# Filter spectra in memory as slot pairs instead of channel chunks, in a two-layer graph kernel on one core

## The reference

```python
# layer 0
norm  = (sum(adj, -1) + 1e-6) ** -0.5
f_hom = (adj @ ((x @ theta) * norm)) * norm
gate  = sigmoid(x @ W_t + b_t)
x     = layernorm(x + elu(gate * f_hom + (1 - gate) * (x @ W_h)))
# layer 1, xc = x with nodes last
h      = relu(bn1(conv1d(xc, conv1_w, 0)))
h      = bn2(conv1d(h, conv2_w, 8))          # 256 -> 256 channels, 17 taps
x_conv = relu(h + xc)
...                                          # A = exp(-dist), x_nmp = A @ relu(x @ w_msg.T + b_msg)
x      = layernorm(x + gru(concat(x_conv, x_nmp), x))
```

## Time and profile before

| | |
|---|---|
| median of 3 runs | 2163.93 us (2160.73 to 2166.66) |
| the profiled execution | 2163.51 us, span 2161.7 us |
| phase_a | from 0 to about 545 us |
| phase_spectrum | about 545 to 767 us |
| phase_product | about 767 to 985 us |
| phase_c | about 985 us to the end |

### The profile page before, as it was taken

One profiled execution on the slowest core, in us unless ns is written; L12 is line 12 of the kernel. 1 busy time (PEld: TensorE's weight loads), 2 busy tenths in 40 slices (PEclk: granted clock), 3 DMA queues, 4 the chain that ended last, 5 costly groups with the idle time before them and its releaser, 6 DMA issues.

```text
span 2161.7 us, 36678 instructions
## 1 busy us (share of the span) xinstructions
PE 1971.6 (91%) x11270; PEld 1695.5 (78%) x11270; DVE 1583.6 (73%) x2837; ACT 1245.1 (58%) x2303; POOL 425.1 (20%) x370
## 2 busy tenths in 40 slices
PE   6888888887788879994999999999999999999997
PEld 5887777776688868883888888888888888888886
DVE  5999798798577766774777677777777777777674
ACT  6887687786455566663445454545454545545452
POOL 5887687685000000000000000000000000000000
PEclk9999999998899989996999999999999999999999
DMA  4556566555322268884212121212122121212110
GB/s 145 204 200 209 192 225 218 198 207 218 91 82 79 72 207 263 255 265 152 76 52 92 46 91 45 91 46 90 60 77 77 59 81 55 88 49 91 62 40 20
DMA packets 174943, 263.25 MB, mean 122 GB/s; under 512 B 13250, under 2 KB 125608, under 8 KB 170632
## 3 DMA queue, kind: packets, MB, share of 16 engines
q1 hardware_dynamic: 174856, 262.29, 35.9%
HBM read 174.16 MB, written 88.08 MB: 121 GB/s over the span
## 4 chain that ended last, share of the span: by engine, by line
PE 51%; issue 1%; DVE 1%; DMA 1%; ACT 1%; SPq 0%; POOLq 0%; POOL 0%; ACTq 0%; DVEq 0%
PE c_ps_g L1431 37%; PE c_ps_m L1412 4%; PE c_ps_s L1412 2%; PE c_ps_m L1440 2%; PE c_ps_y L1466 1%; PE c_ps_m L1442 1%; PE c_ps_y L1510 1%; PE c_ps_m L1510 1%; PE c_ps_s L1494 1%; PE c_ps_m L1441 1%; DMA c_yf<-y_spec 1%; PE c_ps_m L1511 0%; PE c_ps_y L1511 0%; DVE c_wi_l L1377 0%; ACT c_yo L1143 0%
## 5 line engine op out<-in xcount | busy, mean ns | idle before, releaser
L1215 POOL TENSOR_TENSOR c_rstd<-c_var_eps,c_neg_half 128x4 f32<-128x4 f32 x32 | 32.2, 1008 | 1131.7 <-DVE c_var_eps L1331 1131.7
L1431 PE MATMUL c_ps_g<-c_xh,c_wh_l 128*128 128x512 f32 x384 | 155.3, 405 | 0.0
L1431 PE MATMUL c_ps_g<-c_nh,c_wi_l 128*128 128x512 f32 x384 | 153.3, 399 | 0.0
L1431 PE MATMUL c_ps_g<-c_xl,c_wh_h 128*128 128x512 f32 x384 | 151.8, 395 | 0.0
L1431 PE MATMUL c_ps_g<-c_xh,c_wh_h 128*128 128x512 f32 x384 | 151.7, 395 | 0.0
L1431 PE MATMUL c_ps_g<-c_ch,c_wi_l 128*128 128x512 f32 x384 | 151.6, 395 | 0.0
L1431 PE MATMUL c_ps_g<-c_ch,c_wi_h 128*128 128x512 f32 x384 | 151.6, 395 | 0.0
L1431 PE MATMUL c_ps_g<-c_nh,c_wi_h 128*128 128x512 f32 x384 | 151.5, 395 | 0.0
L1431 PE MATMUL c_ps_g<-c_cl,c_wi_h 128*128 128x512 f32 x384 | 151.5, 395 | 0.0
L1431 PE MATMUL c_ps_g<-c_nl,c_wi_h 128*128 128x512 f32 x384 | 151.5, 395 | 0.0
L837 PE MATMUL m_ps<-m_wh,m_xl 128*128 128x256 f32 (+1 forms) x406 | 131.8, 325 | 20.7 <-DVE m_wl L817 20.6
(11 more groups left out here) (228 smaller groups left out, 6658.9 us busy)
## 6 DMA issues: line engine op xcount, KB each, us to landing
w_spec<-a_spec SPq DMA_DIRECT2D x32, 1088.0 KB, 11.0
m_w<-w_spec SPq DMA_DIRECT2D x34, 1024.0 KB, 7.5
a_xt<-in_x_t SPq DMA_DIRECT2D x64, 256.0 KB
a_xn<-in_x_n SPq DMA_DIRECT2D x64, 256.0 KB, 9.4
x_t<-a_x1t SPq DMA_DIRECT2D x64, 256.0 KB, 9.5
s_x<-x_t SPq DMA_DIRECT2D x64, 256.0 KB, 3.0
y_spec<-m_y SPq DMA_DIRECT2D x64, 256.0 KB, 5.6
c_x<-x_t SPq DMA_DIRECT2D x32, 512.0 KB, 4.1
```

Of the source, the lines that this page charges most:

```text
L1431: last = nc.tensor.matmul(out, stationary, moving, start=(count == 0), stop=(count == total - 1))
```

## The change

The scratch tensor becomes (34 pairs of slots, 128 partitions, 8 chunks, 256). A load of two slots is then one run of 8 x 256 floats (8 KB) for each partition. A piece of `a_spec` is no longer one run: each of its pairs of slots is a run of 256 floats (1 KB), and the runs of one partition lie 1 MB apart in HBM, those of neighbouring partitions 8 KB. The pieces hold 9, 9, 8 and 8 pairs of slots in place of four times 8.5. The bytes, the number of DMAs, their place in the program and their waits stay.

```diff
     PIECES = 4
-    PL = L // PIECES
+
+    BOUNDS = (0, 9, 18, 26, SLOTS // 2)
...
                     reached(sp, s_gw, 4 * (p + 1))
-                    sp.dma_start(w_spec[bass.ds(2 * k - half, 1), :, piece * PL:piece * PL + PL].rearrange("o p d c -> (o p) d c"),
-                                 spec[:, half, piece * PL:piece * PL + PL]).then_inc(s_spec[half], 16)
+                    pairs_of = slice(BOUNDS[piece], BOUNDS[piece + 1])
+                    sp.dma_start(w_spec[pairs_of, :, bass.ds(2 * k - half, 1)].rearrange("s p o c -> p s (o c)"),
+                                 spec[:, half].rearrange("p (s d) c -> p s (d c)", d=4)[:, pairs_of]).then_inc(s_spec[half], 16)
...
                     reached(sp, s_wl, i - BUFS + 2)
-                    sp.dma_start(w[:, u % BUFS // 2].rearrange("p t q s r c -> p (t q) (s r c)"),
-                                 w_spec.rearrange("n p d c -> p n d c")[:, :, bass.ds(2 * i, 4)].rearrange("p n d c -> p n (d c)")
-                                 ).then_inc(s_w[u % BUFS // 2], 16)
+                    sp.dma_start(w[:, u % BUFS // 2].rearrange("p t q s r c -> p (t q s r c)"),
+                                 w_spec[bass.ds(k * (UNROLL // 2) + u // 2, 1)].rearrange("o p n c -> (o p) (n c)")).then_inc(s_w[u % BUFS // 2], 16)
...
-    w_spec = nc.dram_tensor("w_spec", (KD * CHUNKS, P, L, CW), F32, kind="Internal").ap()
+    w_spec = nc.dram_tensor("w_spec", (SLOTS // 2, P, KD * CHUNKS, 4 * CW), F32, kind="Internal").ap()
```

## The result

The changed kernel takes 2170.55 us (median of 10 runs, 2167.78 to 2175.69) against 2163.94 us (median of 10) before: a ratio of 1.0032, 95% interval 1.002 to 1.0044. It is 6.6 us slower, 0.3%: little, but the interval leaves out 1. The profiled execution has a span of 2167.6 us, 5.9 us more than that of before.

What follows compares the result with a forecast made beforehand. Phase_a was taken to be bound by its DMA queue, standing on two full engines, and phase_product by PE. From 2163.5 us, +21 for stores and -9 for loads gave 2175 us; own range 2164.5 to 2185.5, whole range near 2157 to 2192.

Steps and rivals of the forecast that it cites:

- Phase_a stands on two full DMA engines: Phase_a: goes at the pace of two DMA engines kept full by 34-row loads, 65.4 us for eight steps against compute's 60.4.
- The price of a fine store: Phase_a: each of 32 `a_spec` stores in 1 KB runs costs +0.65 us, +21 us in all (+11 to +28).
- The growth of ACT's waits for `a_x1t`: Phase_a: ACT's waits for the store of `a_x1t` to land grow above 11.6 us.
- The loads: Phase_product: 34 loads in 8 KB runs land sooner and cut PE's waits, -9 us (at most -10, at least -1).
- Compute's pace as the bound: Phase_a: the queue isn't the bound, only the tail's four stores grow by 2.6 us; 2157 us in all, chance 0.17.
- Run length making no difference: Stores and loads: from 1 KB up run length doesn't matter, nothing changes, 2163.5 us; chance 0.08.
- Scattered writes: Phase_a stores: runs 1 MB apart cost more, +1.20 us a store, +38 us; 2192 us in all, chance 0.13.

Runs made afterwards that it cites:

- the taps spread: Three 34-row loads of taps made one of 112 rows: the kernel before then takes 2141.70 us, the changed kernel 2142.54 us.
- the bare queue: Kernel without compute, issuing phase_a's DMAs alone with the queue kept full: 9.39 us a step with long-run stores, 9.43 with 1 KB runs.

## Why the prediction was right in sign, and where its sizes failed

**Phase_a stands on two full DMA engines: right, shown.** Taking the 34-row loads off them frees 22 us, and 0.66 us put on all engines in each store comes out whole. The Trainium skill, "DMA: Bandwidth & Descriptors", section on why a DMA increments its semaphore by 16, has a rule that makes it two engines for 34 rows; the trace agrees, with 47 to 55 GB/s at a share of 0.1 and none of it with 112 rows.

**The price of a fine store: wrong size.** The term was "+0.35 to +0.86 us a store. I take +0.65", +21 us in all. Phase_a grew by 7.2 us, 0.22 a store. The step that failed took the rate of 1 KB traffic, which is right for a queue of stores alone (0.61 us measured), and put it on a queue where loads and stores alternate. There it is 0.04 us. In the tail, where the stores do stand nearly alone, four of them cost 2.5 us, 0.6 each, as priced; with the taps spread, 1.9 us between the same two points. The DMA view of the changed kernel from 530 to 550 us shows why the price holds there: all sixteen engines are full at the rate of short stores alone, some 350 GB/s, until 2 us before the phase ends.

```profile
DMA  5929999999999999999999999999999999995000
```

The other 4.7 us came in the 28 stores before it, 0.17 each, more than the 0.04 of the bare queue. With the full engines gone these 4.7 us are gone as well. What in the running kernel makes a short store cost more than in the bare queue stays open; the 3 to 4 us for which SP is held behind each, in a kernel where SP must also wait for ACT and POOL, are a candidate that no run singles out. The growth of ACT's waits for `a_x1t` came as forecast.

**The loads: wrong.** The term was -9 us, phase_product gave 0.2. "The landing of 7.5 us should fall to about 6.5" is the step that failed: it is 7.6, and PE's waits are 7.9 us where they were to fall below 2. The 0.81 us on which it rests is the wrong size: with loads and stores mixed, as in this phase, the long runs are worth 0.30 us a load in a full queue (377 and 406 GB/s) and 0.19 us in one that is emptied before each load (231 and 237), and phase_product, at 266 GB/s, lies between. That even these 0.2 to 0.3 us don't show in the landing isn't explained. I had named a landing that is latency and not transfer as the least gain of 1 us, and this least gain is the one that came near. The 317 GB/s on which I built the saving was no rate of the transfer but bytes over a share. A share doesn't measure that: with 8 KB loads phase_product has the same 266 GB/s at 0.83, and loads of 8 KB one at a time show 209 GB/s at 0.59, 354 at full share, where a full queue moves 423.

The stores were priced 14 us too high and the gain of the loads 9 us too high. The two misses offset each other, so that the sum of +12 came out at +6.6; that this lies well inside the range is luck. The sign isn't: it follows from the stores, whose term had the right direction. The range had a slip too: its upper end took 6 us off for the loads, though their least gain was put at 1 us.

**The rivals.** Compute's pace as the bound: refuted. Run length making no difference: with a full queue of loads or of stores alone it is refuted, though nearly true in phase_a's mixed traffic. The Trainium skill, "DMA: Bandwidth & Descriptors", Specifications, puts the least size for line rate at 512 B; 342 and 348 GB/s for 1 KB runs against 420 and 423 for long ones disagree with it, and the measurement decides. Scattered writes: refuted, 342 GB/s both 1 MB and 1.25 KB apart. The rule on row pitches in the Trainium skill, "DMA: Bandwidth & Descriptors", latency and other measured facts, is on the distance from partition to partition, which is 8 KB here; no run here tests it.

## What to carry to other kernels

Before a transfer is priced, ask whether its queue is full and what runs beside it: a rate measured with a full queue says little about a single load on an idle one, and a rate of stores alone little about stores among loads. Bytes over a DMA share are no rate either. A DMA share of 0.12 that comes back in every step was two engines of sixteen with all the work; look first for the transfer whose row count differs from the rest (34 here), for spreading it was worth 23 us and the layout 7. Moving short runs from loads to stores can pay only where someone waits for the loads' bandwidth, and in phase_product PE waited 9 us in all.

## What the hardware showed that I had not expected

Loads and stores of 1 KB runs in turn moved 377 GB/s, while loads alone moved 348 and stores alone 342. Behind a store in 1 KB runs on a busy queue SP stayed 3.5 to 3.8 us in its next issue, behind one in long runs 0.6 to 0.7 us. In phase_a's mix a store of 1.1 MB in 1 KB runs cost 2.82 us of queue (9.43 - 6.61), less than the 3.26 us it costs alone, and one in 8.7 KB runs cost 2.78, more than its 2.65.
